# Attention 0 written out: value products one turn later, another order of projections, more buffers

## The reference, cut to what matters

```python
def _L0_attn_ref(x, w_qkv, w_out):
    H, D, window_size = (16, 64, 32)
    xn = rms_norm(x)
    q, k, v = split(xn @ w_qkv.T)              # heads of 64
    q = apply_rope(q, cos, sin)
    k = apply_rope(k, cos, sin)
    attn = einsum('bhqd,bhkd->bhqk', q, k) / sqrt(D)
    mask = (q_pos >= k_pos) & (q_pos - k_pos <= window_size)
    attn = softmax(where(mask, attn, NEG))
    out = einsum('bhqk,bhkd->bhqd', attn, v)
    return out.reshape(B, T, H * D) @ w_out.T
...
h = _layernorm(x) * (1 + ca) + sa
x = x + ga * _L0_attn_ref(h, ...)
h = _layernorm(x) * (1 + cb) + sb
x = x + gb * _L0_ffn_ref(h, ...)               # router, 8 experts, chosen tokens
...                                            # layer 1: full attention, FP4 feed-forward
```

## Time and profile before

| | us |
|---|---|
| median of 3 runs (lowest, highest) | 1268.82 (1268.05, 1271.76) |
| the profiled execution | 1270.58 |
| its span | 1268.6 |
| of it attention 0, opening left out | 43 to 605 |
| TensorE busy | 966.3 (76%) |
| VectorE busy | 806.4 (64%) |
| ScalarE busy | 638.8 (50%) |
| GpSimd busy | 432.7 (34%) |

### The profile page before, as it was taken

How to read it: one execution, slowest core, us unless ns; L and a number is a source line. 1 busy time by engine, 2 the same in 40 slices (tenths; PEclk the granted TensorE clock), 3 DMA queues, 4 the chain that set the end, 5 groups by cost and what they waited for, 6 DMA issues and landing times. The chain is left out here.

```text
span 1268.6 us, 24925 instructions
## 1 busy us (share of the span) xinstructions
PE 966.3 (76%) x8589; PEld 653.3 (51%) x8589; DVE 806.4 (64%) x1713; ACT 638.8 (50%) x2132; POOL 432.7 (34%) x332
## 2 busy tenths in 40 slices
PE   5889898999989999997613797568158887867675
PEld 3447566565656565656603564335125454535454
DVE  5776867777676758573687551121146878569995
ACT  3565776767676767673101331213048777643322
POOL 2334333324233333230100878776510312200221
PEclk8789899999999999997556898879659999888867
DMA  7574354444344444440402134435310000000000
GB/s 207 146 186 101 86 121 99 117 99 113 82 113 103 113 102 111 108 99 17 142 4 64 46 83 68 66 64 126 33 59 1 2 1 2 1 1 9 17 17 25
DMA packets 89011, 93.64 MB, mean 74 GB/s; under 512 B 18801, under 2 KB 62305, under 8 KB 88945
## 3 DMA queue, kind: packets, MB, share of 16 engines
q1 hardware_dynamic: 78576, 84.14, 25.9%
q0 software_dynamic: 10368, 8.66, 4.7%
HBM read 24.38 MB, written 10.70 MB: 28 GB/s over the span
## 5 line engine op out<-in xcount | busy, mean ns | idle before, releaser
L836 POOL TENSOR_TENSOR qk_cos<-qk_raw,const 128x512 f32<-128x512 f32 x128 | 184.3, 1441 | 312.8 <-ACT qk_raw L590 312.8
L576 ACT ACTIVATE prob<-psS,neg_max 128x96 f32<-128x96 f32 x512 | 167.5, 341 | 85.9 <-DVE neg_max L671 85.1
L443 PE MATMUL psQ<-a_xnT,weights 128*128 128x512 f32 x250 | 148.2, 677 | 1.8 <-ACT a_xnT L622 1.0
L551 PEld LDWEIGHTS psO<-probT,v_windows 96*64 96x64 f32 x2048 | 73.2, 142 | 140.8 <-ACT probT L650 118.9
L551 PE MATMUL psO<-probT,v_windows 96*64 96x64 f32 x2048 | 91.2, 234 | 41.4 <-ACT probT L650 41.2
L686 DVE TENSOR_TENSOR qk_roped<-qk_cos,qk_swapped 128x512 f32<-128x512 f32 x128 | 118.6, 927 | 5.9 <-DVE qk_swapped L677 5.5
L1509 POOL DMA_INDIRECT sums<-ex_y,ex_index x64 | 97.8, 1528 | 29.5 <-issue 18.3
L576 ACT ACTIVATION_READ_ACCUMULATOR prob<-psS,neg_max 128x1 f32 x512 | 105.4, 206 | 0.0
L1498 POOL DMA_INDIRECT ex_rows<-rows,ex_index x64 | 68.2, 1065 | 106.4 <-DMA ex_index<-lists 87.2
L1443 ACT ACTIVATE ex_hidden<-ex_psH,ex_b 128x512 f32<-128x512 f32 x64 | 43.5, 687 | 113.4 <-PE ex_psH L1402 59.4
L650 ACT COPY probT<-psT 96x512 f32<-96x512 f32 x128 | 76.7, 599 | 46.3 <-PE psT L531 46.3
(11 more groups left out here) (319 smaller groups left out, 1999.6 us busy)
## 6 DMA issues: line engine op xcount, KB each, us to landing
qk_swapped<-qk_raw SPq DMA_DIRECT2D x512, 64.0 KB, 2.0
v_windows<-v_tok SPq DMA_DIRECT2D x32, 384.0 KB, 4.3
v_windows<-v_tok SPq DMA_DIRECT2D x32, 256.0 KB, 3.5
mod<-mod_rows SPq DMA_DIRECT2D x12, 512.0 KB, 7.0
ex_w<-in_L_ffn_W SPq DMA_DIRECT2D x16, 256.0 KB, 3.0
v_windows<-v_tok SPq DMA_DIRECT2D x32, 96.0 KB, 2.1
rows<-rt_h SPq DMA_DIRECT2D x8, 256.0 KB, 2.4
sums<-rt_zeros SPq DMA_DIRECT2D x8, 256.0 KB, 2.7
```

What stands on the lines that cost most here:

```text
L443: last = nc.tensor.matmul(bank, k.wqkvT[:, col:col + P], xnT[:, :], start=True, stop=True)
L551: ins = nc.tensor.matmul(psO[D * j:D * j + D, i * P + a * HALF:i * P + (a + 1) * HALF], vw[:, par, a, t, hd], probT[:, 2 * j + i, a * HALF ...
L576: last = nc.scalar.activation(prob[:, s, 2 * j + i, :], psS[:, s, j, i * KW:(i + 1) * KW], ACT.Exp, bias=nmax[:, s, 2 * j + i:2 * j + i + ...
L836: nc.gpsimd.tensor_tensor(rcos[:, half, :], raw[:, half, :], k.const[:, K_COS:K_COS + T], ALU.mult).then_inc(cos_done, 1)
```

## The change

In attention 0:

- All loops are written out, so the waits compare with constants. The router's and the experts' loops are written out as well, and their indices are constants.
- TensorE's order in a turn is: transposes of u, scores of u + 2, value products of u - 1, and then the pieces. The value products of turn 15 stand inside the out-projection, between six of its eight head pairs and the last two.
- `VALUE` is (2, 5) and `HALF_AT` (0, 1, 3, 4): values are projected in t = 0 and t = 2, and the halves one turn further ahead than before; one of them now belongs to the quad three ahead in t = 3.
- ScalarE copies the probabilities first, then the pieces of turn u - 1, then makes the exponentials, then copies the products of u - 1. The squares stand in turn 3, the copy of the turned input in turn 6.
- VectorE's normalisation, modulations, mean squares and scaling stand one turn earlier, GpSimd's root as well (turn 4). The input is turned in turn 6.
- probT, v_tok and xnT have two buffers each; the first two lie in the space of the tensor mod1, and so the trace may name them mod or mod1. `v_placed` is one semaphore for each buffer.
- The out-projection and the turned input use bank 1 of psQ in place of bank 0.
- SP lays out windows in t = 1, behind the swap.

```diff
-        OPENING = [(0, m) for m in (0, 1, 2, 4, 3, 5)] + ["wo0", "wo1"] + [(1, m) for m in (0, 1, 2, 4, 3, 5)]
+        OPENING = [(0, m) for m in range(PIECES)] + ["wo0", "wo1"] + [(1, m) for m in range(PIECES)] + [(2, 0)]
...
-        VALUE = (3, 5)
-        PLAN = ((0,), (1,), (2, 3), (4, 5))
...
-        def turns(eng, body):
-
-            body(0, False)
-            with eng.Fori(1, B - 1) as b:
-                body(b, False)
-            body(B - 1, True)
+        VALUE = (2, 5)
+        HALF_AT = (0, 1, 3, 4)
+        PLAN = (((2, 1), (2, 2)), ((2, 3),), ((2, 4), (2, 5)), ((3, 0),))
+
+        def turns(body):
+
+            for b in range(B):
+                body(b, b == B - 1)
...
+            def apply(b, u):
+
+                g, t = divmod(u, TILES)
+                wait(pe, probT_ready, b * UNITS + u + 1)
+                wait(pe, oT_ready, b * UNITS + u)
+                if t == 0:
+                    wait(pe, v_placed[g % 2], b * 96 + (g // 2 + 1) * 48)
...
             def body(b, last):
                 for u in range(UNITS):
...
+                    turn_prob(b, u)
                     if not (last and u + 2 >= UNITS):
                         score(b, u + 2)
-                    pieces = pieces_at(g, t, last)
+                    if u > 0:
+                        apply(b, u - 1)
                     if u == 0:
                         wait(pe, y_read, b)
-                    if u == 8 and not last:
-                        wait(pe, xnT_ready, b + 2)
-                    for q, m in pieces[:1]:
+                    if u == 6 and not last:
+                        turn_x(b + 1, (b + 1) * QUADS * PIECES - 2)
+                    for q, m in pieces_at(u // TILES, u % TILES, last):
+                        if u == 6 and m == 5 and not last:
+                            wait(pe, xnT_ready, b + 2)
                         project(b, q, m)
...
                 made = QUADS * PIECES if last else (QUADS + 2) * PIECES
-                wait(pe, piece_out, b * QUADS * PIECES + made - 1)
+                wait(pe, piece_out, b * QUADS * PIECES + made)
                 wait(pe, oT_ready, b * UNITS + 3 * TILES)
                 out_project(b, list(range(PAIRS - 2)), True, False)
+                apply(b, UNITS - 1)
                 wait(pe, oT_ready, b * UNITS + UNITS)
                 out_project(b, [PAIRS - 2, PAIRS - 1], False, True)
...
+            def copy_probT(b, u):
+                wait(act, turned, b * UNITS + u + 1)
+                nc.scalar.copy(probT[:, u % 2, :, :], psT[0:KW, :, :]).then_inc(probT_ready, 1)
...
             def body(b, last):
                 for u in range(UNITS):
-                    g, t = divmod(u, TILES)
+                    copy_probT(b, u)
+                    if u > 0:
+                        pieces(b, u - 1, last)
+                    if u == 6 and not last:
+                        copy_xnT(b + 1)
+                    if not (last and u + 2 >= UNITS):
+                        exps(b, u + 2)
                     if u > 0:
                         copy_oT(b, u - 1)
...
-                    if u == 4 and not last:
+                    if u == 3 and not last:
                         squares(b + 1)
-                    if u == 7 and not last:
-                        copy_xnT(b + 1)
+                pieces(b, UNITS - 1, last)
                 copy_oT(b, UNITS - 1)
...
+                        if u == 0:
+                            scaled = own.mark(norm.normalise(dve, own, b + 1, h[:, :, :]))
                         if u == 1:
-                            scaled = own.mark(norm.normalise(dve, own, b + 1, h[:, :, :]))
-                        if u == 2:
...
-                    if u == 5 and not last:
+                    if u == 4 and not last:
                         root(b + 1)
...
                     g, t = divmod(u, TILES)
-                    if t == 0 and not (last and g + 1 >= QUADS):
-                        wait(sp, oT_ready, b * UNITS + g * TILES)
-                        windows(g + 1)
                     q, half = ahead(u, 8)
                     if not (last and q >= QUADS):
                         swap(b, q, half)
...
+                    if t == 1 and not (last and g + 1 >= QUADS):
+                        wait(sp, oT_ready, b * UNITS + g * TILES)
+                        windows(g + 1)
```

More of the change, by code:

```diff
@@ L57, in wait @@
 def wait(engine, sem, value):
-    if not (isinstance(value, int) and value <= 0):
+    if value > 0:
         engine.wait_ge(sem, value)
@@ L586, in piece_from @@
                 if m not in VALUE:
-                    half = half_of(m)
-                    if not (isinstance(b, int) and b == 0 and q == 0):
+                    half = HALF_AT.index(m)
+                    if not (b == 0 and q == 0):
                         wait(act, roped, b * HALVES * QUADS + HALVES * (q - 1) + half + 1)
@@ L593, in piece_from @@
                     if first == 0:
-                        wait(act, v_placed, (b * QUADS + q) * 48)
-                    ins = nc.scalar.copy(v[:, first:first + 2, :], bank.rearrange("p (t d) -> p t d", t=2))
+                        wait(act, v_placed[q % 2], b * 96 + (q // 2) * 48)
+                    ins = nc.scalar.copy(v[:, q % 2, first:first + 2, :], bank.rearrange("p (t d) -> p t d", t=2))
                 ins.then_inc(piece_out, 1)
@@ L613, in squares @@
                 wait(act, h_ready, b + 1)
-                if not (isinstance(b, int) and b == 0):
+                if not (b == 0):
                     wait(act, square_done, b)
@@ L833, in cosines @@
             def cosines(b, q, half):
-                first = isinstance(b, int) and b == 0 and q < 2
-                wait(pool, piece_out, b * QUADS * PIECES + q * PIECES + ((1, 2, 3, 4) if first else (1, 2, 3, 5))[half])
+                wait(pool, piece_out, b * QUADS * PIECES + q * PIECES + HALF_AT[half] + 1)
                 nc.gpsimd.tensor_tensor(rcos[:, half, :], raw[:, half, :], k.const[:, K_COS:K_COS + T], ALU.mult).then_inc(cos_done, 1)
@@ L868, in swap @@
             def swap(b, q, half):
-                first = isinstance(b, int) and b == 0 and q < 2
-                wait(sp, piece_out, b * QUADS * PIECES + q * PIECES + ((1, 2, 3, 4) if first else (1, 2, 3, 5))[half])
+                wait(sp, piece_out, b * QUADS * PIECES + q * PIECES + HALF_AT[half] + 1)
                 for n in range(4):
@@ L966, in phase_router, with pairs @@
         block = ctx.enter_context(nc.Block())
-        def pairs(eng, body):
-            for b in range(2):
-                body(b, b)
-            with eng.Fori(1, B // 2) as pair:
-                for i in range(2):
-                    body(pair * 2 + i, i)
+        def pairs(body):
+            for b in range(B):
+                body(b, b % 2)
         @block.tensor
@@ L1086, in _ @@
                 body(b, b)
-            with dve.Fori(1, B // 2) as pair:
+            for pair in range(1, B // 2):
                 own.turn(pair, OWN_FIRST)
@@ L1352, in phase_experts, with turns @@
         block = ctx.enter_context(nc.Block())
-        def turns(eng, body):
-            for e in range(2):
-                body(e, e, 0, True, False)
-            with eng.Fori(1, E0 // 2 - 1) as pair:
-                for i in range(2):
-                    body(pair * 2 + i, i, pair, False, False)
-            for e in range(E0 - 2, E0):
-                body(e, e % 2, E0 // 2 - 1, False, True)
+        def turns(body):
+            for e in range(E0):
+                body(e, e % 2, e // 2, e < 2, e >= E0 - 2)
         @block.tensor
```

165 lines of the change are left out of this document (75 added, 90 removed).

## The result

The changed kernel takes **1315.22 us** (median of 4 runs, 1310.29 to 1320.14) against 1269.84 for the kernel before on the same chip: a ratio of **1.0339** (95% interval 1.0306 to 1.0373), some 45 us slower. The prediction said 1261.5, with a range up to 1274. The profiled execution has a span of 1308.5, 39.9 more than before.

The account below looks back on a forecast made before the run. VectorE's ring with ScalarE's exponentials, 3.31 us a step, was taken as the bound. 1270.58 - 7.4 (passes 1 to 6) + 1.6 (passes 0 and 7) - 1.7 (router) = 1263.1; less 1.76 to the median, 1261.5; range 1250 to 1274.

Parts of the forecast that it names:

- opening and pass 0: Start of attention 0: earlier work in pass 0 is caught by later waits; its longer end loses 0.8 us.
- the race: Turns t = 1: whether VectorE's rope or GpSimd's cosine starts first; cosine first costs the step 0.93 us.
- the clock: TensorE's granted clock, read as 1.00 in pass 3; the forecast sum gave it no term.
- The ring as the bound: Attention 0: reciprocal, division, sines, maxima, ScalarE's exponentials, next reciprocal set the beat, 3.31 us a step undisturbed.
- the races of u = 1 and 5: Rope against cosine in these two turns, taken as lost: 1.86 us a pass together.
- The extras: VectorE's normalisation, modulations, statistics, mean squares and scaling, one turn earlier: 1.13 us a pass left, bounds 0 and 4.4.
- The race of u = 9 and 13: Rope against cosine in these steady turns: rope taken as first by 0.01 us, so steps take 4.03.
- D: D(u): start of VectorE's reciprocal in turn u, taken as the beat of the pass.
- rival (a): Cosine starts ahead of the rope in u = 9 and 13 too: 11.2 us more, 1272.5 us; chance 0.28.
- The end of the pass: Out-projection cut in two by the last value products, second part waiting for their copy: loss 1.1 us a pass.
- Router: Loop written out: normalise, scale and shift sequences get shorter, gain 1.7 us, between 0 and 2.8.
- Windows: SP's windows behind the swap have a whole turn to land: 0 us; otherwise a quad's first value products would wait.

Follow-up runs that it names:

- the kernel with the rope first: The changed kernel plus one wait: GpSimd's cosine of turn t = 1 waits until VectorE's rope of that turn is done; 1265.88 us, ratio 0.9921.
- the kernel with TensorE kept busy: The changed kernel plus one useless projection for TensorE in each turn t = 2, ahead of the value products; 1282.2 us, ratio 1.0061.
- the kernel with rope, root and end: The changed kernel with rope behind maxima, GpSimd's root back in turn 5, last value products behind four out-projection pairs; 1250.75 us, ratio 0.983.

## Why the prediction was wrong

For an execution like the profiled one the forecast was 1263.1, and 1310.3 came. The 47 us, rounded, from the stretches above: 18.1 are the clock in passes 2 to 6, 9.6 mostly the two races there that were forecast as won (346.1 less five passes of 67.3), 10.9 opening and pass 0, 4.9 pass 1 (3.7 of it the clock), 1.0 the last pass, and 3.1 what lies behind attention 0. Two steps of the prediction failed above all: the race, and the clock, which had no term.

- **The ring as the bound, and its steps: right.** Where no race and no clock interferes, the steps of the changed kernel are 3.30 (u = 3), 3.66 (u = 4), 3.31 (u = 8, 10 to 12) where I had 3.31, 3.65, 3.31, and the races of u = 1 and 5 were lost at 4.97 and 4.98 (5.0 forecast). The extras cost 1.2 a pass in the kernel with the rope first (1.13 forecast). Its clean pass takes 66.3; with u = 1 lost as I had assumed it would be 67.25, and the forecast was 67.3.
- **The race of u = 9 and 13: the wrong side of a sum that was too coarse.** I had the cosine at D + 1.42 and the rope at D + 1.41. It came at D + 1.28, because the copy of the probabilities started 0.13 behind D and not 0.26. TensorE's timeline in the changed kernel, pass 4, from the value products to the transposes:

```profile
399.84 0.69 PE L540 MATMUL psO<-mod,v_windows 96*64 96x64 f32 x16 [0.16 <-ACT oT L629]
400.45 1.12 PE L442 MATMUL psQ<-a_xnT,weights 128*128 128x512 f32 x2
401.41 1.03 PE L447 MATMUL psQ<-weights,a_xnT 128*128 128x256 f32 x4
402.28 0.60 PE L526 MATMUL psT<-const,prob 128*96 128x128 f32 x4
```

  From start to start the half takes 0.96 and the V projection 0.87. I took 1.06 and 0.97 from the earlier trace rows, where other instructions stood behind them: start-to-start times hold only for the pair from which they were read. That made 0.2 too much, and the products started 0.1 later than I had (0.38 behind D). The mechanism of rival (a) was right, and its price nearly (1.00 for a lost race, 0.93 forecast): its pass was 67.3 + 1.9 = 69.2, and the kernel with TensorE kept busy shows this pass, 69.2.
- **What a lost race does to TensorE's clock: the step that was missing.** The sum had no term for it, in the forecast or in any rival. I had read the clock at 1.00 in the earlier trace rows and took it as given, though the change leaves TensorE a wait of 1.42 behind each lost race. The sign was there to be read: passes 5 and 6 of before show 0.98, with the fall behind a wait of 1.46. Price 18.1 us in passes 2 to 6 alone: the largest single term. Rival (a) by itself, 1272.5, lies within the range; with this term more it would be 1290.6.
- **Opening and pass 0: 0.8 where 11.7 came.** Of the 3.1 in the opening 1.9 arise ahead of the projections, in work that the change leaves as it was: the first half starts at 20.3 in place of 18.3, behind the same twelve products that took 2.82 in place of 1.53; in four of the five other kernels with this opening it starts at 18.1 to 18.3. In pass 0 the later waits did not absorb the earlier normalisation as I said. I priced it at 1.10 as in the earlier trace rows, which holds in passes 2 to 6 (1.11); in pass 0 it had the root of the same turn in front of it and two cosines beside it. How the 8.6 of pass 0 divide among this, lost races and the clock (0.86 for 0.89) stays open.
- **The end of the pass: about right.** The out-projection takes 8.66 in place of 7.31, +1.35 for the 1.1 forecast; from D(14) it is 5.58 where the clock holds (5.8 forecast), and 7.2 where it fell.
- **Router: right.** From its first root to its softmax 28.7 in place of 30.5; 1.7 forecast. Experts: unchanged, as said. Windows: 0 in the changed kernel, as said; once a pass is faster, SP's issues come late, and it is the sines that wait for swapped rows (1.52 in the kernel with rope, root and end), not the value products as I had it.
- The sentence from the Trainium skill, "SBUF — State Buffer", section "Who interferes with whom", that the order of issue decides who blocks, is what these runs show: 0.69 against 1.70 for the same rope by 0.12 us of lead, and back to 0.69 with one wait.

## What to carry to other kernels

Where two engines contend and the order of starting decides, a margin of a few hundredths of a microsecond is no forecast: put the order into the program with a wait, or put the instruction where losing costs nothing, as behind the maxima here. A stall priced only by its own length can be priced too low when TensorE idles behind it: look at what it ran just before and after, and ask what the same work takes at the lower clock. And a useless product in a known gap is a cheap experiment that parts the two.

## What the runs showed of the hardware

- An idle stretch of TensorE of 1.42 us in otherwise full work was followed by the lower clock (0.50) for some three to seven us in ten of twenty cases in the changed kernel, in three of ten in the kernel with the rope first, and, at 1.46 us, in two of five in the kernel before and in none of five when that is written out; with 1.13 us of that time filled, in none of twenty.
- SP issued a transfer every 0.64 to 0.72 us (means of three windows and of sixteen swaps), whatever its size here (64 to 384 KB); a quad's 19 take about 13 us.
- A normalisation of four 128x128 instructions (one tensor input from SBUF) took 3.01 beside two cosines and 1.10 without: it was not only the sums of two tensors that took longer beside GpSimd.
